# Four reads of scan states on GpSimd instead of VectorE, large loads held back, and new orders on all engines

## The chip, the cores and the metric

One Trainium2 chip, one of its cores. The metric is the device time of one execution in microseconds, taken as the median of several. The core has a matmul engine (TensorE, "PE" in the profile, its weight loads "PEld"), VectorE ("DVE"), ScalarE ("ACT"), GpSimd ("POOL") and SyncE ("SP", which here only issues transfers). Every engine runs its own list of instructions in the order in which it was written; semaphores tie the lists together.

## What is computed

Eight sequences of 256 tokens with 128 channels go through four layers, each followed by "add the input and normalize":

```python
x = _layernorm(x + attention(x))   # L0: linear attention, decay k, state kv by a scan over time
x = _layernorm(x + x @ W[idx] + b[idx])                    # L0 ffn, one expert out of 8
x = _layernorm(x + metric_attention(x))                    # L1: proj, gram, mixer
x = _layernorm(x + ffn(x))                                 # L1: silu(x w1)*(x w2), gelu(h1), gelu(h2), w3

# the attention of L0
k = sigmoid(x @ key_w.T + key_b); v, q = split(x @ vq_w.T)
upd = (1.0 - k)[..., :, None] * v[..., None, :]            # per head 8 x 8
_, kv = associative_scan(combine, (k[..., :, None], upd), axis=1)
h = einsum('nthd,nthde->nthe', q, kv);  return h @ out_w.T + out_b
```

The expert index comes from the logits and a noise vector, so its weights can only be fetched once a short chain of tiny operations is done.

## The kernel before

The 2048 tokens are cut into four groups (a, b, c or g = 0 to 3) of 512 columns, two sequences each. A group passes through these steps, and the groups overlap: while one group is in the last layer's feed-forward part, the next are still in the attention.

- **Attention, for each of eight value channels e.** TensorE spreads one row of value differences over 128 partitions (`replicate(a, e)`, bank `rep_bank`, two of them in turn). VectorE scans it over time (`scan(a, e)`: two instructions of 256 columns, into one of four buffers of `state`). The result is multiplied by the query (`read_state(a, e)`, 128x512, both inputs in SBUF, into one of four buffers of `read`). TensorE multiplies it with the output weights (`attend(a, e)`, eight matmul rows in the profile, summed in `y1_bank`). `direct_product(a)` and `attend_direct(a)` close the sum. `value_steps(a)`, `high_values`/`low_values(a, i)` make the value differences and split them in two parts. A scan may start when the read four steps back has ended (`STATES = 4`), a read when the attend four steps back has.
- **Normalization n of group g** (n = 0 to 2 inside, 3 at the end): `norm_sum`, `norm_stats`, `norm_moments`, `norm_varied` on VectorE, `inverse_std` on GpSimd (a power on 128x4, rows `rstd<-varied,power`), `norm_shift` on VectorE, `norm_out` on ScalarE (four tiles of 128 columns) for groups 0 and 1, on VectorE later. TensorE transposes the four tiles as they come (`transposes(g, n)`).
- **Expert layer.** VectorE and ScalarE take turns in `routing` and `route_on(0..7)`; after `route_on(7)` SyncE fetches `chosen_w` and `chosen_b`, GpSimd adds the identity (`passed_weights`), TensorE multiplies (`routed(b)`), and `norm_sum(1, b)` follows.
- **Metric layer.** `heads_of`, `gram_of`, `mask_gram`, `mix`, `through_metric`, `residual_of_metric`, `metric_out` go to and fro between TensorE, ScalarE and VectorE, then `norm_sum(2, b)`.
- **Feed-forward.** After `transposes(b, 2)`, ScalarE copies the high part (`high_x3`), VectorE takes the low part (`low_x3`), and TensorE runs `gate_of`/`up_of(c, m)` (rows with `x3T_high`, `x3T_low`), two hidden layers `hidden(c, layer, m)` of eight matmuls each, and `narrow(c)`, `turn_back(c)`. Every operand is in a high and a low part; GpSimd makes some of the low parts (`low_product`, `low_gelu`). The table of silu and that of gelu are loaded on ScalarE at each change (`ACT_TABLE_LOAD`).

GpSimd also adds the bias to the input (`attend_residual(a)`, row `res<-xt,attend_pack`), which needs the tokens `xt` from a transfer. SyncE issues all loads at the start in one go, and the reloads of `xt` later. In `without_weights()` TensorE does the work ahead of the first feed-forward matmul, in `with_weights()` the rest. The order of each engine is a list of calls at the end of its block: the four lists decide everything about who waits for whom.

## Time and profile before

| | us |
|---|---|
| median of 3 runs | 200.31 |
| lowest, highest | 199.05, 201.71 |
| profiled execution, whole | 198.95 |
| its span, first to last instruction | 197.2 |
| TensorE busy | 178.5 (91%) |
| VectorE busy | 143.8 (73%) |
| ScalarE busy | 124.7 (63%) |
| GpSimd busy | 63.9 (32%) |

A row of the timeline reads: start, duration, engine, line of the kernel, operation, output and inputs, and in brackets the idle time just before and what ended it. Rows of pipelined engines overlap by some 0.08 us, so what an instruction costs its engine is the distance of two starts, not the duration shown.

### The profile page before, as it was taken

To read this page: it belongs to the slowest core of one execution; us is meant where nothing else is said; L and a number is where in the kernel's file an instruction comes from. 1 tells how busy PE (TensorE), PEld (TensorE's weight loads), DVE (VectorE), ACT (ScalarE), POOL (GpSimd) and SP (SyncE) were. 2 spreads that over 40 slices of the span, in tenths; PEclk is the share of its full clock that TensorE was granted. 3 is DMA by queue.
4 is the path that set the end of the run, shared out by engine and by line. 5 is a ranking of instruction groups with operands and counts; after the bars stand their busy time and mean duration, and the time that the engine had idled before them with its cause. 6 is when DMAs were issued, how large, how long until landed. Compare 5 with 4: busy or idle time off the path is not lost.

```text
span 197.2 us, 2885 instructions
## 1 busy us (share of the span) xinstructions
PE 178.5 (91%) x949; PEld 140.4 (71%) x949; DVE 143.8 (73%) x375; ACT 124.7 (63%) x207; POOL 63.9 (32%) x61
## 2 busy tenths in 40 slices
PE   7797999698799999999999999999999999899940
PEld 7454685385697687997789889987678886576830
DVE  0699999989799999499779991777860545803572
ACT  3879972845304797635884663467877569885630
POOL 0020001420001152843504234490516572465511
PEclk9999999998899999999999999999999999999997
DMA  4998000210000000100000000000000100001102
GB/s 118 243 421 366 3 2 22 76 38 3 0 0 0 2 3 0 49 8 0 0 0 2 3 0 0 0 0 0 3 2 0 53 5 0 0 6 48 53 3 57
DMA packets 6704, 7.83 MB, mean 40 GB/s; under 512 B 544, under 2 KB 5664, under 8 KB 6432
## 3 DMA queue, kind: packets, MB, share of 16 engines
q1 hardware_dynamic: 6688, 7.63, 11.7%
q8 instruction: 9, 0.15, 0.3%
q14 instruction: 7, 0.06, 0.1%
HBM read 6.58 MB, written 1.05 MB: 39 GB/s over the span
## 4 chain that ended last, share of the span: by engine, by line
PE 56%; issue 15%; DVE 9%; ACT 9%; DMA 3%; POOL 3%; SPq 2%; POOLq 0%; DVEq 0%; ACTq 0%
PE c_bank L1386 33%; PE y_bank L1291 6%; PE b_bank L1320 6%; DMA xt<-x_tok 3%; ACT normed_lent L417 3%; PE b_bank L1347 2%; DVE state L832 2%; PE b_bank L1315 2%; SPq L239 1%; POOL res L293 1%; DVE stats L875 1%; PE b_bank L1386 1%; DVE read L842 1%; ACT gate L528 1%; PE sum_bank L1386 1%
## 5 line engine op out<-in xcount | busy, mean ns | idle before, releaser
L832 DVE TENSOR_TENSOR_SCAN state<-rep_bank,keep 128x256 f32<-128x256 f32 x62 | 38.8, 673 | 0.3 <-PE rep_bank L1278 0.3
L305 POOL TENSOR_TENSOR rstd<-varied,power 128x4 f32<-128x4 f32 x15 | 15.2, 1010 | 62.5 <-DVE varied L889 62.5
L1291 PEld LDWEIGHTS y_bank<-attend_pack,read 128*128 128x128 f32 x256 | 31.5, 192 | 5.0 <-DVE read L842 2.6
L1291 PE MATMUL y_bank<-attend_pack,read 128*128 128x128 f32 x256 | 33.1, 277 | 0.5 <-DVE read L842 0.3
L842 DVE TENSOR_TENSOR read<-state,query 128x512 f32<-128x512 f32 x32 | 22.4, 707 | 0.1
L314 POOL TENSOR_TENSOR hid_odd_low<-hid,hid_odd_high 128x512 fp32r<-128x512 f32 x12 | 15.7, 1311 | 20.2 <-ACT hid L545 20.1
L545 ACT ACTIVATE hid<-c_bank,scales_pack 128x512 f32<-128x512 f32 x31 | 21.0, 682 | 0.0
L1386 PE MATMUL c_bank<-hid_even_high,hidden_rounded 128*128 128x512 f32 x64 | 19.4, 414 | 0.5 <-ACT gate L528 0.5
L1386 PE MATMUL c_bank<-hid_odd_low,hidden_rounded 128*128 128x512 f32 x64 | 18.6, 400 | 0.5 <-DVE hid_odd_low L985 0.5
L1386 PE MATMUL c_bank<-hid_odd_high,hidden_rounded 128*128 128x512 f32 x64 | 18.7, 404 | 0.2 <-ACT hid L545 0.2
L539 ACT ACTIVATE hid_even_high<-c_bank,scales_pack 128x512 fp32r<-128x512 f32 x15 | 10.3, 688 | 13.2 <-PE c_bank L1386 13.1
L539 ACT ACTIVATE hid_odd_high<-c_bank,scales_pack 128x512 fp32r<-128x512 f32 x16 | 11.0, 688 | 11.8 <-PE c_bank L1386 11.6
L1386 PE MATMUL c_bank<-hid_even_low,hidden_rounded 128*128 128x512 f32 x64 | 18.4, 396 | 0.0
L309 POOL TENSOR_TENSOR hid_even_low<-hid,hid_even_high 128x512 fp32r<-128x512 f32 x8 | 10.2, 1283 | 21.0 <-ACT hid_even_high L534 21.0
L1386 PEld LDWEIGHTS c_bank<-hid_odd_low,hidden_rounded 128*128 128x128 f32 x64 | 12.0, 187 | 4.2 <-DVE hid_odd_low L985 1.4
L1386 PEld LDWEIGHTS c_bank<-hid_even_high,hidden_rounded 128*128 128x128 f32 x64 | 11.6, 189 | 3.9 <-ACT gate L528 0.9
L1386 PEld LDWEIGHTS c_bank<-hid_even_low,hidden_rounded 128*128 128x128 f32 x64 | 12.0, 188 | 3.2 <-DVE hid_even_low L980 0.4
L1386 PEld LDWEIGHTS c_bank<-hid_odd_high,hidden_rounded 128*128 128x128 f32 x64 | 11.5, 188 | 2.6 <-ACT hid L545 0.4
L417 ACT ACTIVATE normed_lent<-normed_lent,shift,rstd 128x128 f32<-128x128 f32 x16 | 6.6, 482 | 7.4 <-DVE shift L895 7.4
L314 POOL TENSOR_TENSOR hid_even_low<-hid,hid_even_high 128x512 fp32r<-128x512 f32 x8 | 10.3, 1293 | 2.5 <-ACT hid L545 2.5
L534 ACT CAST hid_even_high<-hid 128x512 fp32r<-128x512 f32 x16 | 9.7, 619 | 2.1 <-DVE hid L975 1.9
L293 POOL TENSOR_TENSOR res<-xt,attend_pack 128x512 f32<-128x512 f32 x4 | 5.6, 1408 | 15.0 <-DMA xt<-x_tok 13.1
(188 smaller groups left out, 361.7 us busy)
## 6 DMA issues: line engine op xcount, KB each, us to landing
hidden_pack<-hidden SPq DMA_DIRECT2D x2, 1024.0 KB, 10.5
xt<-x_tok SPq DMA_DIRECT2D x4, 256.0 KB, 2.8
xT_lent<-x_chan SPq DMA_DIRECT2D x3, 256.0 KB, 5.9
mlp_pack<-mlp SPq DMA_DIRECT2D x1, 768.0 KB, 7.7
out<-xT_lent SPq DMA_DIRECT2D x3, 256.0 KB, 2.3
attend_pack<-attend SPq DMA_DIRECT2D x1, 640.0 KB, 4.2
metric_pack<-metric SPq DMA_DIRECT2D x1, 448.0 KB, 11.8
xT_lent<-x_chan SPq DMA_DIRECT2D x2, 128.0 KB, 2.5
```

The costliest lines, as they stand in the source:

```text
L305: nc.gpsimd.tensor_tensor(rstd[n][:], varied[n][:], power[:], ALU.pow).then_inc(ln_rstd[n], 1)
L309: nc.gpsimd.tensor_tensor(hid_parts[0][1][:, m, :], hid[:, m, :], hid_parts[0][0][:, m, :].bitcast(F32), ALU.subtract).then_inc(low_pool[0 ...
L314: nc.gpsimd.tensor_tensor(hid_parts[layer][1][:, m, :], hid[:, m, :], hid_parts[layer][0][:, m, :].bitcast(F32), ALU.subtract).then_inc(lo ...
L417: nc.scalar.activation(normed[n][:, tile(j)], total[n][:, tile(j)], ACT.Identity, bias=shift[n][:, j:j + 1], scale=rstd[n][:, j:j + 1]).th ...
L534: nc.scalar.copy(hid_parts[0][0][:, m, :], hid[:, m, :]).then_inc(product_high, 1)
L539: nc.scalar.activation(hid_parts[layer][0][:, m, :], c_bank[m % 2][:], ACT.Gelu, scale=scale).then_inc(gelu_high, 1)
L545: nc.scalar.activation(hid[:, m, :], c_bank[m % 2][:], ACT.Gelu, scale=scale).then_inc(gelu_done, 1)
L832: ins = nc.vector.tensor_tensor_scan(state[:, e % STATES, at], rep_bank[e % 2][:, at], keep[:, a * T + s * SEQ:a * T + (s + 1) * SEQ], 0.0 ...
L842: nc.vector.tensor_tensor(read[:, e % READS, :], state[:, e % STATES, :], query[:, a * T:(a + 1) * T], ALU.mult).then_inc(read_ready, 1)
L1291: ins = nc.tensor.matmul(y1_bank[:, tile(j)], read[:, e % READS, tile(j)], out_w_rep_sb[:, e, :], start=(e == 0 and j == 0), stop=False, s ...
L1320: ins = nc.tensor.matmul(bank_[:, tile(j)], src[:, tile(j)], w(j), start=True, stop=True)
L1386: return nc.tensor.matmul(bank_[:], weights[exact[0]][k], moving, start=(k == 0 and i == 0), stop=(k == last and i == 1))
```

## The change

GpSimd makes four reads of states: (1, 2), (1, 5), (2, 2) and (2, 5). They have a semaphore of their own, and those who wait for a read ask `read_done` which one to wait for. At the start SyncE issues the tokens of group 0 after the second group's input, waits until that input has landed, and only then issues the remaining inputs, and the weights, `metric` first. A table `ACT_TILES` splits the tiles of `norm_out`; its values leave all four tiles with ScalarE where they were. The lists of calls of all engines are new.

```diff
+ACT_TILES = {(0, 0): 4, (0, 1): 4, (1, 0): 4, (1, 1): 4, (2, 0): 4, (2, 1): 4}
+POOL_READS = ((1, 2), (1, 5), (2, 2), (2, 5))
+        def read_done(a, e):
+            n = sum((i, k) in POOL_READS for i in range(a + 1) for k in range(HD if i < a else e + 1))
+            return (read_ready_pool, n) if (a, e) in POOL_READS else (read_ready, HD * a + e + 1 - n)
             for g in range(1, NG):
                 at = slice(g * T, (g + 1) * T)
                 sp.dma_start(xT[:, at], x_chan[:, at]).then_inc(xT_loaded[g], 16)
-            load_tokens(0)
-            for pack in ("mlp", "hidden1", "hidden2", "metric"):
+                if g == 1:
+                    load_tokens(0)
+                    sp.wait_ge(xT_loaded[1], 16)
+            for pack in ("metric", "mlp", "hidden1", "hidden2"):
                 load_pack(pack)
+            def read_state(a, e):                                    # on GpSimd
+                pool.wait_ge(scan_done, HD * a + e + 1)
+                pool.wait_ge(proj_out, PROJECTIONS * (a + 1))
+                if HD * a + e >= READS:
+                    pool.wait_ge(attended, HD * a + e + 1 - READS)
+                nc.gpsimd.tensor_tensor(read[:, e % READS, :], state[:, e % STATES, :], query[:, a * T:(a + 1) * T],
+                                        ALU.mult).then_inc(read_ready_pool, 1)
 # scan(a, e) on VectorE
-                    dve.wait_ge(read_ready, HD * a + e + 1 - STATES)
+                    dve.wait_ge(*read_done(*divmod(HD * a + e - STATES, HD)))
 # attend(a, e) on TensorE
-                pe.wait_ge(read_ready, HD * a + e + 1)
+                pe.wait_ge(*read_done(a, e))
 # VectorE's list, two of its places
             norm_varied(2, 0)
             norm_sum(0, 1)
             rounding_flag()
+            norm_stats(0, 1)
+            norm_shift(2, 0)
...
 # ScalarE's list, one of its places
+            sum_low_halves(2)
+            round_weights(2)
             norm_out(2, 0)
 # TensorE's list, the start
-                project(3)
                 replicate(0, 1)
                 replicate(0, 2)
+                project(3)
 # TensorE's list, the end
                 narrow_early(0)
+                narrow_early(1)
                 narrow_late(0)
-                narrow_early(1)
+                narrow_late(1)
                 turn_back_last(0)
-                narrow_late(1)
```

The list of GpSimd from the first `inverse_std` on, before. The `res` is `attend_residual(1)`, `passed_w` is `passed_weights`:

```order
L305 TENSOR_TENSOR rstd<-varied,power 128x4
L293 TENSOR_TENSOR res<-xt,attend_pack 128x512
L299 TENSOR_TENSOR passed_w<-chosen_w,metric_pack 128x128
L305 TENSOR_TENSOR rstd<-varied,power 128x4 x3
L309 TENSOR_TENSOR hid_even_low<-hid,hid_even_high 128x512 x2
```

The same place after. The reads stand between the powers of the normalizations:

```order
L347 TENSOR_TENSOR rstd<-varied,power 128x4
L333 TENSOR_TENSOR passed_w<-chosen_w,metric_pack 128x128
L327 TENSOR_TENSOR res<-xt,attend_pack 128x512
L340 TENSOR_TENSOR read<-state,query 128x512
L347 TENSOR_TENSOR rstd<-varied,power 128x4
L340 TENSOR_TENSOR read<-state,query 128x512 x2
L347 TENSOR_TENSOR rstd<-varied,power 128x4 x2
L351 TENSOR_TENSOR hid_even_low<-hid,hid_even_high 128x512
```

`passed_weights` has moved ahead of `attend_residual(1)`, and three reads stand in front of the first low part.

VectorE from the last step of the expert choice to the statistics of normalization 1 of group 0, before:

```order
L771 TENSOR_SCALAR expert<-route 128x1
L875 BN_STATS stats<-total 128x6 x4
L882 BN_AGGR moments<-stats 128x2 x4
L842 TENSOR_TENSOR read<-state,query 128x512
L889 TENSOR_SCALAR varied<-moments 128x4
L832 SCALAR_TENSOR_TENSOR state<-rep_bank,keep 128x256 x2
L895 SCALAR_TENSOR_TENSOR shift<-moments,rstd 128x4
L832 SCALAR_TENSOR_TENSOR state<-rep_bank,keep 128x256 x4
L842 TENSOR_TENSOR read<-state,query 128x512
L813 TENSOR_TENSOR dvalue_first<-dvalue,dvalue_first 64x512
L860 TENSOR_TENSOR normed_lent<-b_bank,chosen_b 128x512
```

After (the two reads in one row are (1, 1) and (1, 3)):

```order
L817 TENSOR_SCALAR expert<-route 128x1
L937 TENSOR_SCALAR varied<-moments 128x4
L888 TENSOR_TENSOR read<-state,query 128x512
L878 SCALAR_TENSOR_TENSOR state<-rep_bank,keep 128x256 x2
L943 SCALAR_TENSOR_TENSOR shift<-moments,rstd 128x4
L853 TENSOR_TENSOR dvalue<-value 128x512
L878 SCALAR_TENSOR_TENSOR state<-rep_bank,keep 128x256 x2
L888 TENSOR_TENSOR read<-state,query 128x512 x2
L878 SCALAR_TENSOR_TENSOR state<-rep_bank,keep 128x256 x2
L908 TENSOR_TENSOR normed_lent<-b_bank,chosen_b 128x512
```

The statistics now come before the last step of the choice, the low part of group 2's values has moved back, and two reads stand where one stood.

TensorE at the change from group 2 to group 3 in the feed-forward part, before (the `normed` transposes are `transposes(3, 2)`, the row of `mlp_rounded` with `hid_even_high` begins `narrow(2)`):

```order
L1315 MATMUL b_bank<-metric_pack,normed_lent 128x128 x4
L1386 MATMUL c_bank<-hid_odd_high,hidden_rounded 128x512 x4
L1386 MATMUL c_bank<-hid_odd_low,hidden_rounded 128x512 x4
L1386 MATMUL sum_bank<-x3T_high,mlp_rounded 128x512
L1386 MATMUL sum_bank<-x3T_low,mlp_rounded 128x512
L1386 MATMUL c_bank<-hid_even_high,mlp_rounded 128x512 x3
```

After:

```order
L1430 MATMUL c_bank<-hid_odd_high,hidden_rounded 128x512 x4
L1430 MATMUL c_bank<-hid_odd_low,hidden_rounded 128x512 x4
L1359 MATMUL b_bank<-metric_pack,normed_lent 128x128 x4
L1430 MATMUL c_bank<-hid_even_high,mlp_rounded 128x512 x3
L1430 MATMUL c_bank<-hid_even_low,mlp_rounded 128x512 x2
L1430 MATMUL c_bank<-hid_even_high,mlp_rounded 128x512
L1430 MATMUL c_bank<-hid_even_low,mlp_rounded 128x512 x2
L1430 MATMUL sum_bank<-x3T_high,mlp_rounded 128x512
```

The transposes stand behind the last hidden tile of group 2 now, and `narrow(2)` ahead of the first gate.

## Rows read from the trace of the kernel before

**Rows 1.** The page's second part: busy tenths in 40 slices of 4.93 us.

```profile
PE   7797999698799999999999999999999999899940
DVE  0699999989799999499779991777860545803572
```

**Rows 2.** Busy time (instructions) of each engine by stretch, then granted clock, DMA share, GB/s.

```profile
44.20:58.80 14.60, 12.64 (x72) 10.18 (x73) 13.08 (x33) 4.68 (x9) 0.00 (x0) 0.88 0.00 1
63.90:101.70 37.80, 37.36 (x206) 30.67 (x207) 32.74 (x81) 27.25 (x48) 15.99 (x13) 1.00 0.03 8
101.70:162.30 60.60, 59.79 (x342) 50.19 (x341) 40.07 (x123) 38.38 (x63) 27.20 (x23) 1.00 0.02 6
```

**Rows 3.** Timeline of VectorE: distance of starts, a wait for TensorE's replicate.

```profile
24.51 0.67 DVE L842 TENSOR_TENSOR read<-state,query 128x512 f32<-128x512 f32 x1
25.09 0.15 DVE L761 TENSOR_REDUCE route<-route 128x1 f32<-128x8 f32 x1
...
11.67 2.44 DVE L832 TENSOR_TENSOR_SCAN state<-rep_bank,keep 128x256 f32<-128x256 f32 x4 [0.29 <-PE rep_bank L1278]
```

**Rows 4.** Timeline of VectorE beside GpSimd, 36 to 40 us and at 80 us.

```profile
37.28 1.07 DVE L842 TENSOR_TENSOR read<-state,query 128x512 f32<-128x512 f32 x1
38.38 0.83 DVE L813 TENSOR_TENSOR dvalue_first<-dvalue,dvalue_first 64x512 fp32r<-64x512 f32 x1
39.91 0.69 DVE L860 TENSOR_TENSOR normed_lent<-b_bank,chosen_b 128x512 f32<-128x512 f32 x1 [0.71 <-PE b_bank L1320]
...
79.74 0.67 DVE L842 TENSOR_TENSOR read<-state,query 128x512 f32<-128x512 f32 x1
...
36.54 1.26 POOL L293 TENSOR_TENSOR res<-xt,attend_pack 128x512 f32<-128x512 f32 x1 [1.75 <-DMA xt<-x_tok]
37.76 0.90 POOL L299 TENSOR_TENSOR passed_w<-chosen_w,metric_pack 128x128 f32<-128x128 f32 x1
...
79.76 1.81 POOL L293 TENSOR_TENSOR res<-xt,attend_pack 128x512 f32<-128x512 f32 x1
```

**Rows 5.** Timeline of SyncE and TensorE around the expert's weights.

```profile
33.26 0.38 SPq L262 DMA_DIRECT2D chosen_b<-ffn_b  x1
...
38.72 1.16 PE L1320 MATMUL b_bank<-passed_w,x1T 128*128 128x128 f32 x8 [1.67 <-POOL passed_w L299]
```

**Rows 6.** TensorE in one microsecond (busy, granted clock), and VectorE's wait for the gram.

```profile
45.00:46.00 1.00, 0.91 (x3) 1.00 0.00 0
48.00:49.00 1.00, 1.00 (x6) 0.50 0.06 16
...
51.36 0.42 DVE L956 TENSOR_TENSOR gram<-b_bank,metric_pack 128x256 f32<-128x256 f32 x1 [1.42 <-PE b_bank L1347]
```

**Rows 7.** Timeline of ScalarE and VectorE where the feed-forward part starts.

```profile
60.30 1.65 ACT L417 ACTIVATE normed_lent<-normed_lent,shift,rstd 128x128 f32<-128x128 f32 x4 [5.76 <-DVE shift L895]
...
63.21 0.66 DVE L966 TENSOR_TENSOR x3T_low<-b_bank,x3T_high 128x512 fp32r<-128x512 f32 x1
```

**Rows 8.** Timeline of TensorE: transposes that wait for tiles, and one that doesn't.

```profile
66.88 1.28 PE L1315 MATMUL b_bank<-metric_pack,normed 128*128 128x128 f32 x4
...
77.33 0.94 PE L1315 MATMUL b_bank<-metric_pack,normed_lent 128*128 128x128 f32 x4
...
160.02 0.60 PE L1315 MATMUL b_bank<-metric_pack,normed_lent 128*128 128x128 f32 x4
```

**Rows 9.** ScalarE and TensorE from group 2 to group 3 of the feed-forward part.

```profile
163.79 1.28 ACT L528 ACT_TABLE_LOAD   x1
...
169.99 1.01 PE L1386 MATMUL c_bank<-hid_even_high,hidden_rounded 128*128 128x512 f32 x3 [0.51 <-ACT gate L528]
```

**Rows 10.** Timeline of ScalarE: the casts of both hidden layers' weights.

```profile
20.45 3.69 ACT L478 CAST hidden_rounded<-hidden_pack 128x2048 fp32r<-128x2048 f32 x2
```

**Rows 11.** Timeline of the last instructions: TensorE's wait, the last power on GpSimd.

```profile
187.87 0.39 PE L1481 MATMUL c_bank<-hid_even_low,mlp_rounded 128*128 128x256 f32 x1 [0.44 <-DVE hid_even_low L915]
...
192.19 0.73 POOL L334 TENSOR_TENSOR rstd<-varied,power 128x2 f32<-128x2 f32 x1 [0.67 <-DVE varied L944]
```

More of the change, by code:

```diff
@@ L713, in _ @@
             silu(3, 1)
-            silu_table(3)
             silu(3, 2)
@@ L1594, in with_weights @@
[L1594 to L1595 removed]
+                replicate(2, 7)
                 attend(2, 4)
+                transposes(1, 1)
                 attend(2, 5)
[L1598 to L1599 removed]
+                heads_of(1)
                 hidden(0, 1, 0)
+                gram_of(1)
                 hidden(0, 1, 1)
[L1602 removed]
+                mix(1)
+                hidden(0, 1, 2)
                 replicate(3, 0)
[L1604 removed]
```

468 lines of the change are left out of this document (238 added, 230 removed).

## The prediction

> **What bounds the kernel now.** I read the busy tenths first. VectorE stands at 9 with few breaks from 10 to 80 us while TensorE has 7s and 8s in between; from 80 us on TensorE stands at 9 to the tail and VectorE falls to 3 to 8 [rows 1]. The table by stretch says the same: from 63.9 to 101.7 us TensorE is busy 37.36 of 37.80, from 101.7 to 162.3 us 59.79 of 60.60 [rows 2]. So there are two halves. Up to the first feed-forward matmul VectorE is the bound (scans and reads), and what lies on its list ahead of `low_x3(0)` (start 63.21 [rows 7]) sets when TensorE's solid half begins. From there TensorE's fixed amount of work sets the end. A microsecond taken from VectorE ahead of 63 us is worth a microsecond if TensorE can be fed in the second half; one taken after is worth little.
>
> Then I read where VectorE stood still or was slow in the first half. It waited 0.29 us at 11.67 for a replicate [rows 3], 0.71 us at 39.91 for `routed(0)` and 1.42 us at 51.36 for the gram [rows 4, 6]. Two instructions ran long: a read of 1.07 us and a low part of 0.83 us [rows 4].
>
> **The sum, first half (up to `low_x3(0)`).**
> - Reads. Of the four, (1, 2), (1, 5) and (2, 2) stood ahead of `low_x3(0)`. A read costs VectorE 25.09 - 24.51 = 0.58 us [rows 3], in dense stretches 0.60; three give 1.8. On GpSimd a 128x512 product of two SBUF operands takes about 1.26 us, as the `res` row does [rows 4], and GpSimd was idle for the whole of 44.2 to 58.8 us [rows 2]. Their users (the scan four steps on, the attend) come over 2 us later in the new list, so the longer read is hidden; without that cover each would cost 0.7.
> - The wait of 0.29. In the new list `replicate(0, 1)` and `(0, 2)` stand ahead of `project(3)`, which waited for the second group's input. Gone: 0.29. I cost the holding back of the large loads at nothing: the input it may speed up is no longer waited for, and the first user of what is held back, ScalarE's cast of the `mlp` weights, feeds only the feed-forward part 40 us later.
> - The wait of 0.71. TensorE waited 1.67 us for `passed_w` until 38.72 [rows 5]; the weights had been asked for at 33.26, but GpSimd had first to wait for the tokens (`res`, 36.54, released by a transfer) [rows 4, 5]. With `passed_weights` in front, it starts some 1.8 us after the request, at 35, and `routed(0)` follows ScalarE's copy at about 36.4. Gone: 0.71.
> - The wait of 1.42. `heads_of(0)` and `gram_of(0)` ran at a granted clock of 0.50 (1.2 GHz, against 1.00 before), after microseconds in which TensorE had little to do [rows 6]. In the new list an attend stands between `transposes(0, 1)` and `heads_of(0)`, and VectorE has two scans, two reads, a direct product and a low part to do ahead of `mask_gram(0)`, where before there was less. Even at the slow clock the gram would be there. Gone: 1.42.
> - Contention as it was: 1.07 - 0.67 and 0.83 - 0.69 = 0.54 [rows 4]. Gone at its old place, since the neighbours change.
> - Against that, `norm_varied` and `norm_shift(0, 1)` now stand ahead of `low_x3(0)`: 0.15.
> - New contention. The read at 37.28 asked while GpSimd's `res` (36.54, 1.26 long) ran, and ended 0.55 us after that one had; at 79.76 it is `res` that takes 1.81 us, behind a VectorE read begun at 79.74 [rows 4]. So of two instructions with two SBUF inputs each, the later waits for the whole of the earlier. The Trainium skill has this as a rule (SBUF — State Buffer, "Who interferes with whom"): a VectorE instruction with two SBUF inputs contends with a GpSimd instruction that reads SBUF, and the loser blocks fully. By that rule the trace agrees, and it speaks against this change. Where does it bite? By the new list, `passed_w` would run about 34.9 to 35.8 and `res` 36.3 to 37.5, while VectorE wants its reads (1, 1) at 35.3 and (1, 3) at 36.3: 0.45 and 1.15. The moved reads mostly face scans, statistics and PSUM operands, which GpSimd doesn't slow; `read(2, 2)` falls together with VectorE's `read(2, 1)`, but starts later and so is the one that waits. I take 1.1, between 0 (VectorE is first each time) and 1.6.
>
> Sum: 1.8 + 0.29 + 0.71 + 1.42 + 0.54 - 0.15 - 1.1 = **3.5 us** (3.0 to 4.6). I set this against the list walked through with the distances of starts: the first shift would come at 33.4, that of normalization 2 at 57 instead of 60.1, and `high_x3(0)` 2.8 to 3.7 us earlier.
>
> **The sum, second half.**
> - `replicate(2, 5)` has moved behind the start: TensorE has 0.24 us more to do.
> - Waits of transposes for ScalarE's tiles. Four transposes take 0.60 as a row when the tiles are there, and took 1.28 at 66.88 and 0.94 at 77.33 [rows 8]; with the small idle pieces and another at 94.67 I count 1.7 us lost by TensorE between 63.9 and 101.7. In the new list `norm_out(1, 1)` comes ahead of the gelus and `norm_shift(1, 1)` some 8 us earlier, so that one goes; `norm_out(0, 1)` still is waited for (0.4), and `norm_out(2, 1)` (0.2). With a reserve I take a gain of 0.8 (0 to 1.2).
> - From group 2 to 3. ScalarE's table load ends at 165.07 and TensorE waits 0.51 for a gate at 169.99 [rows 9]. `high_x3(3)` now stands in that chain (0.6 longer), but TensorE's transposes have moved into the gap (0.36 shorter), and `narrow(2)` covers the copy. I take 0, between -0.6 and 0.4.
> - The tail. `narrow_early(1)` fills the 0.44 us that TensorE waited; the chain there runs on VectorE and GpSimd (the last power starts at 192.19) and gains 0.1 [rows 11].
> - Everything between 101.7 and 162.3: TensorE idles 0.81 in all [rows 2]. The new orders could hardly win there; I take nothing.
>
> 3.5 - 0.24 + 0.8 + 0 + 0.1 = 4.16, **4.2 us**. The profiled execution took 198.95 (span 197.2), so it becomes 194.8. That execution is the lowest of four readings (198.95, 199.05, 200.31, 201.71), whose middle is 199.7; from there 195.5, from the median of the runs, 200.31, it would be 196.1. I say **195.5**.
>
> **The rivals.**
> - *Only the reads count.* VectorE is still over 90% busy from 60 to 80 us [rows 1], and the time won at its waits reappears as other waits of the new list, since the chain of layers (shift, ScalarE, transposes, GpSimd) has lengths of its own. Then four reads at 0.6 are left, 2.4, less 0.24: 2.2 us, 197.5 us. For it: half of my gain is waits, and waits move. Against: each has its cause removed by name.
> - *The shared access eats the gain.* Each GpSimd read blocks a VectorE instruction for its whole 1.26 us, and is itself late: 4 x 1.26 = 5.0 against 5.3 (the 4.2 with its 1.1 of contention left out): 199.4 us. Against: VectorE's neighbours there are mostly scans, which ran beside GpSimd unslowed.
> - *The other side: ScalarE in front of the chain.* Before, both casts of the hidden weights were done by 24.1 (3.69 us, [rows 10]). Now one stands ahead of `norm_out(1, 0)` with a table load, the other with its sum of halves between `move_mixed(0)` and `norm_out(2, 0)`: 1.85 + 1.28, and 1.85 + about 1.9 (an estimate: the sum reads as much as the cast). If norm 1's shift comes before 40.3 and norm 2's before 54, they are in the chain; fully exposed that is 6.9 against the 4.2: 202.4, and beyond 2% with a wait of the flag (`flag_sum` needs that sum) on top, 204. Against: ScalarE waited 5.76 us ahead of `norm_out(2, 0)` [rows 7], and by my walk the slack is 2 and 3 us. It decides only from there.
> - *More than I count*: no contention and all waits of the transposes gone, 4.6 - 0.24 + 1.2 + 0.4 + 0.1 = 6.1 us: 193.6.
>
> **Chances.** Forecast (gain 3.2 to 5.2) 0.48; only the reads 0.22; shared access 0.15; ScalarE's side 0.07, of which two thirds beyond 2%; more 0.08. The range reaches from "more" (193.6, and 0.8 below it for the scatter of the four readings) up to the shared access at 199.4. 2%, about what a measurement of this kernel can tell from no change, is a gain of 4.0, just below the forecast: faster 0.50, same 0.45, slower 0.05.
>
> **What would show it.** In the changed kernel's timeline: `passed_w` at 35 and ahead of the second `res`; no VectorE wait above 0.3 us at the gram; GpSimd reads of 1.3 us, VectorE reads of over 1 us only beside `res` or `passed_w`; `norm_out(2, 0)` at about 57 and `high_x3(0)` near 59.5 instead of 62.4; a granted clock of 1.00 from 45 to 52; TensorE busy over 98% from there on. I am wrong if VectorE's reads last over a microsecond at several places, if ScalarE comes to `norm_out(2, 0)` straight from a cast, or if TensorE idles more than 1 us between 60 and 160.

## The result, and the profile after

The changed kernel takes 193.62 us (192.63 to 194.08, four executions) where the kernel before, run beside it, took 200.38 (199.05 to 201.71): a ratio of 0.972, 95% interval 0.967 to 0.977. Run again later, beside the kernel before on one chip, it took 193.77 (192.90 to 195.75, six executions) against 198.68: 0.978 (0.973 to 0.982). One of those seventeen executions of the kernel before took 251.57 us, at a mean granted clock of 0.655, and is left out of the ratio. The profiled execution took 193.92 us, span 192.1; the one before had 198.95 and 197.2.

The busy tenths and the granted clock (the share of its full speed at which TensorE ran), page of the kernel after:

```profile
PE   7779796999999999999999999999899999999930
DVE  0799999999999997679979986668470774804461
PEclk9999999999999999999999999999999999999985
```

TensorE's long row of 9s begins at the 8th slice (34 us) instead of the 12th (54 us); VectorE's has no break from the 3rd to the 15th, where there were two, in the 9th and 11th [rows 1]. The same in windows of the kernel after (busy time and count of PE, PEld, DVE, ACT, POOL, then granted clock, DMA share, GB/s), the three stretches that answer to [rows 2]:

```profile
39.00:53.60 14.60, 13.87 (x101) 11.93 (x99) 14.44 (x36) 8.55 (x13) 3.94 (x3) 1.00 0.02 6
59.20:97.00 37.80, 37.75 (x211) 31.49 (x212) 32.69 (x76) 27.82 (x49) 14.74 (x13) 1.00 0.03 8
97.00:155.80 58.80, 57.87 (x332) 48.42 (x331) 42.21 (x122) 37.05 (x60) 28.19 (x23) 1.00 0.02 6
```

In the first one VectorE is busy 14.44 of 14.60 (13.08 before) and the clock is 1.00 (0.88 before); in the second TensorE idles 0.05 us where it idled 0.44.

The timeline of GpSimd and VectorE in the kernel after, where [rows 4] and [rows 6] were:

```profile
34.42 0.46 POOL L333 TENSOR_TENSOR passed_w<-chosen_w,metric_pack 128x128 f32<-128x128 f32 x1 [1.83 <-DMA chosen_b<-ffn_b]
35.83 1.34 POOL L327 TENSOR_TENSOR res<-xt,attend_pack 128x512 f32<-128x512 f32 x1 [0.94 <-DMA xt<-x_tok]
37.12 1.28 POOL L340 TENSOR_TENSOR read<-state,query 128x512 f32<-128x512 f32 x1
...
34.65 1.38 DVE L888 TENSOR_TENSOR read<-state,query 128x512 f32<-128x512 f32 x2
37.14 0.66 DVE L908 TENSOR_TENSOR normed_lent<-b_bank,chosen_b 128x512 f32<-128x512 f32 x1
46.72 0.40 DVE L1004 TENSOR_TENSOR gram<-b_bank,metric_pack 128x256 f32<-128x256 f32 x1
```

The weights come ahead of the residual and take 0.46 us instead of 0.90; neither `norm_sum(1, 0)` (37.14) nor the gram's mask (46.72) has a wait behind it. At the start of the feed-forward part, ScalarE and VectorE, for [rows 7]:

```profile
55.41 1.65 ACT L463 ACTIVATE normed_lent<-normed_lent,shift,rstd 128x128 f32<-128x128 f32 x4 [3.24 <-DVE shift L943]
...
58.45 0.69 DVE L1014 TENSOR_TENSOR x3T_low<-b_bank,x3T_high 128x512 fp32r<-128x512 f32 x1
```

`low_x3(0)` starts at 58.45 instead of 63.21, 4.76 us earlier. Then TensorE at the turn from group 2 to 3 and the last power on GpSimd, for [rows 8, 9, 11]:

```profile
156.34 0.60 PE L1359 MATMUL b_bank<-metric_pack,normed_lent 128*128 128x128 f32 x4
...
161.05 0.50 PE L1430 MATMUL c_bank<-x3T_high,mlp_rounded 128*128 128x512 f32 x1 [0.42 <-ACT gate L612]
...
186.58 0.73 POOL L376 TENSOR_TENSOR rstd<-varied,power 128x2 f32<-128x2 f32 x1 [0.23 <-DVE varied L992]
```

The lead at the last power is 5.61 us; the span shows 5.1.

**Where the two ends of an execution lie.** To compare profiles of many kernels one has to leave out two stretches that differ from execution to execution of one kernel. Ahead, VectorE's first scan starts when the first transfers and ScalarE's copies are done: at 8.18 us here, at 9.00 in a second profile of the same kernel. Behind, the output's last transfer: from the end of VectorE's last instruction to the end of the span it took 4.15 us here and 2.22 in that second profile. So the table counts from the start of the first scan; all figures are starts on VectorE's timeline (the scan reads `sum_bank`; the last instruction is the last scaling of `xT_lent`).

| kernel | first scan at | to `low_x3(0)` | to last instruction | span |
|---|---|---|---|---|
| before | 8.49 | 54.72 | 184.47 | 197.2 |
| old orders, four reads on GpSimd | 8.27 | 54.53 | 184.32 | 196.8 |
| new orders, all reads on VectorE | 8.05 | 55.56 | 185.52 | 197.6 |
| the same, spare matmuls at 22 us | 8.20 | 53.05 | 183.03 | 194.1 |
| after | 8.18 | 50.27 | 179.17 | 192.1 |
| after, second profile | 9.00 | 50.42 | 179.28 | 191.1 |
| after, spare matmuls at 22 us | 8.24 | 50.18 | 179.08 | 191.5 |
| after, loads as before | 8.33 | 51.55 | 180.42 | 191.6 |
| after, five more reads on GpSimd | 10.28 | 49.98 | 179.30 | 193.5 |
| after, heads ahead of the attend | 8.41 | 52.96 | 181.83 | 194.0 |
| after, turn 2 to 3 as before | 8.22 | 50.21 | 180.23 | 192.6 |
| before, attend between | 8.65 | 53.72 | 183.48 | 196.7 |
| before, spare matmuls at 45 us | 8.03 | 54.14 | 183.88 | 196.5 |
| before, weights first | 8.17 | 53.74 | 183.54 | 196.2 |

Seven of these fourteen profiles, the one of the kernel before among them, hold a fall of TensorE's granted clock ahead of `low_x3(0)`: about 1 us of a difference between two rows can be that and nothing else.

Before to after that is 4.45 us in the first half, 0.85 in the second, 0.31 at the start, and 0.52 given back behind the last instruction: 5.1 in the span.

### The profile page after: what moved, and what is told of

It is laid out like the page before. It is cut to its first block and busy times, and to the rows that moved or that the text cites. A ratio compares the mean times of both kernels' runs of the same rounds, so it can differ in the third digit from the quotient of the medians.

```text
span 192.1 us, 2885 instructions
## 1 busy us (share of the span) xinstructions
PE 173.9 (91%) x949; PEld 138.1 (72%) x949; DVE 143.7 (75%) x371; ACT 124.9 (65%) x207; POOL 69.6 (36%) x65
## 3 DMA queue, kind: packets, MB, share of 16 engines
HBM read 6.58 MB, written 1.05 MB: 40 GB/s over the span
## 5 line engine op out<-in xcount | busy, mean ns | idle before, releaser
L347 POOL TENSOR_TENSOR rstd<-varied,power 128x4 f32<-128x4 f32 x15 | 15.9, 1063 | 57.0 <-DVE varied L937 57.0
L888 DVE TENSOR_TENSOR read<-state,query 128x512 f32<-128x512 f32 x28 | 20.8, 754 | 0.0
L1322 PE MATMUL rep_bank<-dvalue_second,rep_r 128*128 128x512 f32 x16 | 8.3, 524 | 2.2 <-DVE state L878 1.5
```

The costliest lines, as they stand in the source:

```text
L347: nc.gpsimd.tensor_tensor(rstd[n][:], varied[n][:], power[:], ALU.pow).then_inc(ln_rstd[n], 1)
L888: nc.vector.tensor_tensor(read[:, e % READS, :], state[:, e % STATES, :], query[:, a * T:(a + 1) * T], ALU.mult).then_inc(read_ready, 1)
L1322: nc.tensor.matmul(rep_bank[e % 2][:], rep_r[:, e, :], dvalue_parts[a % 2][e // (HD // 2)][:], start=True, stop=True).then_inc(rep_ready, 1)
```

## The experiments

**Reads alone, orders alone.** First the four reads on GpSimd in the old lists, with the loads as before:

```diff
 # VectorE's list, four places
-            read_state(1, 2)
 # GpSimd's list
             passed_weights()
+            read_state(1, 2)
             inverse_std(1, 0)
+            read_state(1, 5)
+            read_state(2, 2)
...
             inverse_std(0, 1)
+            read_state(2, 5)
```

> The lists of the kernel before, with only the four reads moved to GpSimd (in the places that suit that list); loads as before. Theory A (orders make the gain: each VectorE wait ends at a fixed event of another engine, so a read taken away ahead of a wait only makes the wait longer): reads (1,2) and (1,5) are swallowed by the waits at 39.9 and 51.4, (2,2) counts 0.6: low_x3(0) starts at about 62.6 instead of 63.2, time 0.6 us under the kernel before (ratio 0.997). Theory B (only the reads count, 0.6 us each): low_x3(0) at 61.4, time 1.8 to 2.2 us less (ratio 0.989). Theory C (shared access of VectorE and GpSimd eats it): no gain or a loss, ratio 1.00 to 1.01, VectorE instructions of over 1 us beside the GpSimd reads.

198.03 us, ratio 0.993 (0.988 to 0.998). VectorE's timeline in it, for the two waits of [rows 4, 6]:

```profile
39.74 0.69 DVE L905 TENSOR_TENSOR normed_lent<-b_bank,chosen_b 128x512 f32<-128x512 f32 x1 [1.57 <-PE b_bank L1361]
51.18 0.42 DVE L1001 TENSOR_TENSOR gram<-b_bank,metric_pack 128x256 f32<-128x256 f32 x1 [2.02 <-PE b_bank L1388]
```

The waits of 0.71 and 1.42 have become 1.57 and 2.02 (both profiles have the clock down at 48 us), and there is a new one of 0.29 at `low_x3(0)`, for ScalarE. VectorE does 1.8 us less and stands 1.75 us longer; in the profile 0.2 us is left at `low_x3(0)`. The freed time is swallowed where VectorE waits for others. That is one execution of each kernel. Over all of them the gain is larger: a ratio of 0.993 of 199 us is 1.3 us, with an interval from 0.4 to 2.3, so it lies between the 0.6 of theory A and the 2.2 of theory B and excludes neither.

Then the new lists and the held loads, with the four reads back on VectorE:

```diff
-POOL_READS = ((1, 2), (1, 5), (2, 2), (2, 5))
+POOL_READS = ()
 # VectorE's list, one of four places
             read_state(1, 1)
+            read_state(1, 2)
             read_state(1, 3)
```

> The changed kernel with the four reads given back to VectorE, all else new. Theory A: VectorE of the changed kernel has no wait between 10 and 58 us, so three reads ahead of low_x3(0) cost it their full 0.6 each: low_x3(0) at 60.2 instead of 58.45, the time 1.8 us above the changed kernel (about 195.4 where that has 193.6; ratio to the kernel before 0.981). Theory B (orders bring nothing without the reads): back to the time of the kernel before, ratio 0.995 to 1.0. Theory C (the reads on GpSimd cost as much as they save): the same time as the changed kernel, ratio 0.972.

199.08 us, ratio 0.998 (0.993 to 1.002): nothing of the gain can be told from noise. What was lost is more than the 1.8 us of the three reads on the path, and the trace names a cause that I had not thought of. TensorE's attends and VectorE in this kernel, then the windows of TensorE's clock:

```profile
24.46 4.57 PE L1335 MATMUL y_bank<-attend_pack,read 128*128 128x128 f32 x24
...
29.96 0.69 DVE L911 TENSOR_TENSOR total<-y_bank,res 128x512 f32<-128x512 f32 x1 [1.30 <-PE y_bank L1342]
...
22.00:24.00 2.00, 0.59 (x2) 0.31 (x2) 2.00 (x6) 2.00 (x3) 0.00 (x0) 1.00 0.08 25
24.00:26.00 2.00, 1.92 (x11) 1.60 (x12) 2.00 (x5) 1.71 (x4) 0.00 (x0) 0.77 0.01 4
26.00:28.00 2.00, 2.00 (x11) 2.00 (x11) 2.00 (x5) 0.00 (x0) 0.00 (x0) 0.50 0.00 0
```

TensorE has little to do from 22 to 24 us (busy 0.59 of 2.00), its clock then reads 0.77 and 0.50 (1.2 GHz instead of 2.4 for most of three microseconds), 24 attend matmuls take 4.57 us (3.03 in the changed kernel's profile), and VectorE waits 1.30 for their result. At 46 to 48 us the clock reads 0.50 again. Of its ten executions eight have a mean clock of 0.967 to 0.977, lower than any of the changed kernel's.

**Does the clock do it?** Six spare matmuls in TensorE's gaps, their result used by nobody; the same edit in this kernel and in the changed one:

```diff
+            def keep_busy():
+                for _ in range(2):
+                    nc.tensor.matmul(b4_bank[:, 0:P], ones[:], ones[:], start=True, stop=True)
 # TensorE's list
+                keep_busy()
                 replicate(1, 0)
+                keep_busy()
                 replicate(1, 1)
+                keep_busy()
                 attend(0, 5)
```

> New orders with the four reads on VectorE, and the same six spare matmuls in the gap at 22 to 24 us. Without them this kernel had clock 0.77 and 0.50 from 24 to 28, `attend(0, 5..7)` in 4.57 us, and `norm_sum(0, 0)` waited 1.30 us for TensorE; `low_x3(0)` came at 63.61. Theory Clock: 1.00 from 24 to 28, that wait under 0.2, `low_x3(0)` near 62.2, time about 197.6 (ratio 0.991). What is left against the changed kernel (some 3.5 us) is then the price of the reads themselves and of the second dip at 46 to 50. Rival: the dip comes from something else; times as without the spare matmuls, 199 and ratio 0.998.

> The changed kernel with six spare 128x128 matmuls of the constant `ones` on TensorE, two each ahead of `replicate(1, 0)`, `replicate(1, 1)` and `attend(0, 5)`, where TensorE has the three short waits around 22 to 24 us (0.66 and 0.68 us in the changed kernel's trace). Their result is not used. Theory Clock: with TensorE only 0.96 busy in the 2 us from 22, the granted clock stands at an edge; in the run with the old loads the same gap was followed by 0.60 and 0.54, and the 24 matmuls of `attend(0, 5..7)` took 4.57 us where they take 3.03. Spare work in the gap keeps the clock at 1.00, the scatter between executions shrinks, and the median falls by some 0.5 us (as if no execution had the dip, worth about 1.3). Rival: the clock does not follow the gap, or VectorE is the bound there anyway; the spare matmuls (about 0.24 us each) then cost 0 to 0.5 us, same clock in the runs as before.

With the reads on VectorE: 197.53 us, ratio 0.994 (0.990 to 0.998), against 199.08 without the spare work. Its TensorE timeline:

```profile
24.27 2.84 PE L1339 MATMUL y_bank<-attend_pack,read 128*128 128x128 f32 x24
```

4.57 has become 2.84 and the wait of 1.30 is gone. So the wait was the slow clock. That the spare matmuls kept the clock up is likely and not shown by the profile alone: in the one without them the `mlp` weights had also landed later (18.57 instead of 17.93), VectorE had waited 0.58 us for what is queued behind them, and part of TensorE's thin stretch came from that (0.96 busy of the 2 us in the changed kernel, 0.59 here). The profile with them is also of the fastest of its ten executions, 195.85. The mean clocks of all executions say more: eight of ten are at 0.977 or below without the spare work, two of ten with it. In the changed kernel the window answering to the one above is

```profile
22.00:24.00 2.00, 1.54 (x10) 1.15 (x9) 2.00 (x6) 1.98 (x3) 0.00 (x0) 1.00 0.05 12
```

(0.96 busy without the spare work). It took 193.35 us, four executions within 193.27 to 193.66, ratio 0.972 (0.965 to 0.979). In the profile it is 0.1 us shorter than the changed kernel, which had no fall of the clock in its own profile either. The narrow spread is what the theory asked for, but the median is not apart from 193.62 or 193.77, and with no fall in the profile of either there is nothing here that the spare work can be seen to prevent.

The two kernels with spare matmuls have no fall ahead of `low_x3(0)` and no wait of VectorE between its first scan and there. They give the price of the reads in the new lists: 53.05 to 50.18 at `low_x3(0)`, 2.87 us, and 183.03 to 179.08 at the end, 3.95 us. Three reads at 0.60 are 1.8 of the 2.87. The rest stands on two rows of the kernel with the reads on VectorE:

```profile
34.67 2.95 DVE L884 TENSOR_TENSOR read<-state,query 128x512 f32<-128x512 f32 x3
...
35.75 1.32 POOL L327 TENSOR_TENSOR res<-xt,attend_pack 128x512 f32<-128x512 f32 x1 [1.09 <-DMA xt<-x_tok]
...
69.00 1.23 DVE L939 SCALAR_TENSOR_TENSOR shift<-moments,rstd 128x4 f32<-128x4 f32 x1
```

Reads (1, 1), (1, 2) and (1, 3) take 2.88 us from start to start instead of 1.8, because the last of them meets GpSimd's `res`: 1.08 us of shared access. With (1, 2) moved away VectorE has two reads there and is out before it matters (1.31 us in the profile of after, 1.20 in the one with spare matmuls). So the moved read takes its own 0.6 and a meeting of 1.1 with it. Behind `low_x3(0)` there is the fourth read, and a step of 128x4 that lasts 1.23 instead of 0.16 beside a GpSimd product (third row).

In the old lists the same four reads were worth 0.2 in the profile. And the new lists without them are worth 1.4 (184.47 to 183.03). 0.15 and 1.44 make 1.6; together they made 5.3. (The 1.44 and the 5.3 both hold about 1 us that the kernel before lost in its profile to a fallen clock, below.) These are single executions. By the ratios, the reads alone bring 0.7%, the lists alone 0.2% (0.6% with the spare matmuls), and both together 2.2 and 2.8% in the two comparisons: a smaller disproportion than in the profiles, and still about twice the sum. The change is neither half but the two together.

**The same kernel again.**

> The changed kernel itself once more, beside the others on one chip, for the scatter of its executions: the version with spare matmuls at 22 to 24 us stayed within 193.27 to 193.66. Theory Clock: this one scatters by 1 us or more, with a median 0 to 0.6 above 193.35. Rival: the spare matmuls changed nothing; same median and same narrow spread.

192.90 to 195.75, six executions, median 193.77; mean clock 0.981 to 0.992, the longest at 0.981. The scatter is over 1 us, as expected of it; the median is 0.4 above the one with spare work, on another chip, which settles nothing.

**The loads.** The changed kernel with SyncE's requests in the order before:

```diff
-                if g == 1:
-                    load_tokens(0)
-                    sp.wait_ge(xT_loaded[1], 16)
-            for pack in ("metric", "mlp", "hidden1", "hidden2"):
+            load_tokens(0)
+            for pack in ("mlp", "hidden1", "hidden2", "metric"):
```

> The changed kernel with SyncE's start as it was: nothing held back, tokens after all inputs, mlp before metric. As predicted (holding back is worth nothing): same times to 0.1 us, low_x3(0) at 58.4, the time that of the changed kernel. Rival E (holding back brings the earlier start: the first VectorE scan of pair (0,1) stood at 9.37 in the changed kernel and the first scans 0.5 us earlier than before): the first value steps at 6.5 go back to 7.1, low_x3(0) 0.5 us later, the time 0.5 us more.

193.60 us, ratio 0.974 (0.966 to 0.983): no difference. But its profile isn't the same, it has the fall of the clock, in the same place:

```profile
24.19 4.57 PE L1332 MATMUL y_bank<-attend_pack,read 128*128 128x128 f32 x24
```

VectorE waits 1.30 us for it, which is all of its 1.3 us at `low_x3(0)`. It seems to belong to that execution (mean clock 0.973; the other three have 0.984 to 0.987). The rival of an earlier start falls: the second value step stands at 6.63 with the old loads, at 6.49 and 7.31 in two profiles with the held ones. I had costed the held loads at nothing because ScalarE's cast of the `mlp` weights feeds only the feed-forward part. That overlooks what is queued behind the cast: ScalarE's cast of `dvalue_first`, which VectorE needs for its low part. With the old loads the first cast started at 15.67 without waiting; in the changed kernel it waited 2.01 us, to 17.65, and VectorE's low part found its input with half a microsecond to spare. Two other executions with held loads did not (below).

**More reads.** Five more on GpSimd: (0, 1), (0, 3), (0, 5), (1, 6), (1, 7).

```diff
-POOL_READS = ((1, 2), (1, 5), (2, 2), (2, 5))
+POOL_READS = ((0, 1), (0, 3), (0, 5), (1, 2), (1, 5), (1, 6), (1, 7), (2, 2), (2, 5))
 # GpSimd's list
             attend_residual(0)
+            read_state(0, 1)
+            read_state(0, 3)
+            read_state(0, 5)
...
             read_state(1, 5)
+            read_state(1, 6)
+            read_state(1, 7)
             read_state(2, 2)
```

> The changed kernel with five more reads on GpSimd: (0,1), (0,3), (0,5), (1,6), (1,7), lists otherwise as they are. Theory A (VectorE is the only bound up to 58 us): 5 x 0.6 = 3.0 us less ahead of low_x3(0), which starts at 55.5; the time 3.0 us under the changed kernel, 190.6. Rival D (a second chain, shift - ScalarE - transposes - heads - gram, or TensorE's own list, lies just behind VectorE): VectorE gets waits of together 1.5 us or more, the gain is 0.5 to 1.5 us. Theory C (shared access): GpSimd's nine reads at 1.27 us block VectorE reads, gain below 0.5 us.

194.45 us, ratio 0.975 (0.966 to 0.984). From the first scan on, 50.0 us to `low_x3(0)` and 179.3 to the end, against 50.3 and 179.2: VectorE has 3 us less to do and gets 0.3 of it, for a while. VectorE and GpSimd in this kernel:

```profile
16.55 1.13 DVE L808 TENSOR_SCALAR route<-route 128x8 f32<-128x8 f32 x1
45.61 1.20 DVE L864 TENSOR_TENSOR dvalue_first<-dvalue,dvalue_first 64x512 fp32r<-64x512 f32 x1
47.41 1.27 DVE L883 TENSOR_TENSOR_SCAN state<-rep_bank,keep 128x256 f32<-128x256 f32 x2 [0.60 <-PE rep_bank L1322]
...
15.87 1.77 POOL L340 TENSOR_TENSOR read<-state,query 128x512 f32<-128x512 f32 x1 [1.81 <-DVE state L883]
44.99 1.27 POOL L340 TENSOR_TENSOR read<-state,query 128x512 f32<-128x512 f32 x1 [0.57 <-PE y_bank L1335]
```

A step of 128x8 elements that takes 0.23 us elsewhere lasts 1.13, beside a GpSimd read that itself lasts 1.77; the low part at 45.61 ends 0.55 us behind the read that began at 44.99. Then VectorE waits for TensorE (0.60, and 0.44 at `through`). At these two rows shared access takes 1.4 us of the three; two reads of 0.82 take another 0.3, and the waits 1.0. So the rival I feared is real; it is four reads in the right places that escape it.

**The place of the attend and the clock at 45 to 50 us.** In the changed kernel, the attend moved behind the heads:

```diff
                 transposes(0, 1)
-                attend(1, 3)
                 heads_of(0)
+                attend(1, 3)
```

> The changed kernel with `heads_of(0)` ahead of `attend(1, 3)` on TensorE, so that this attend no longer lies in the wait for ScalarE's copy. Theory A/Clock: TensorE is idle 0.6 us more at 44 to 46, heads wait for the copy either way; the chain is no later (gram within 0.1 of 46.72), the attend moves behind it; the clock is at 1.00 in most executions but dips to 0.50 in some between 46 and 50, a median 0 to 0.6 us above the changed kernel. Rival (the place of the attend is what saved the 1.42 us): the gram waits again by 0.5 us or more in the profile at clock 1.00.

194.54 us (193.84 to 195.91), ratio 0.978 (0.973 to 0.983). From `total(0)` to `low_x3(0)` its profile has 30.52 us, the changed kernel's 30.30: no wait at the gram, at a clock of 1.00. So the attend's place is not what removed it. The median is not apart from the 193.77 of the changed kernel beside it. The profile was of the longest of the four executions; ScalarE and VectorE in it:

```profile
19.56 1.47 ACT L524 CAST mlp_rounded<-mlp_pack 128x1536 fp32r<-128x1536 f32 x1 [3.70 <-DMA mlp_pack<-mlp]
...
21.59 0.69 DVE L859 TENSOR_TENSOR dvalue_first<-dvalue,dvalue_first 64x512 fp32r<-64x512 f32 x1 [1.19 <-ACT dvalue_first L504]
30.85 0.69 DVE L915 TENSOR_TENSOR total<-y_bank,res 128x512 f32<-128x512 f32 x1 [1.19 <-PE y_bank L1342]
```

This is what the held loads can cost: `mlp` landed 1.9 us later than in the profile of after, ScalarE's cast held up the next, VectorE waited 1.19, TensorE starved for it (busy 0.28 of the 2 us from 22, by the windows), its clock fell to 0.50, and VectorE waited another 1.19. The kernel with all reads on VectorE shows the same, smaller: 0.58 us at 20.59.

In the kernel before, the attend put between:

```diff
                 flag_sum()
-                attend(1, 4)
                 replicate(1, 7)
                 transposes(0, 1)
+                attend(1, 4)
                 replicate(2, 0)
                 heads_of(0)
```

> The kernel before, with one move on TensorE: `attend(1, 4)` from ahead of `replicate(1, 7)` to between `transposes(0, 1)` and `heads_of(0)`, where TensorE waits for ScalarE. Theory A (the gram of group 0 waits for TensorE because this attend was in front of the chain): the chain's `heads_of(0)` comes some 0.5 us earlier, VectorE's wait of 1.42 us at the gram falls to 0.5 to 0.9, `low_x3(0)` 0.5 to 0.9 earlier, time 198.3 to 198.6 where before has 199.0. Theory Clock: what makes that wait is the clock of 0.50 at 48 to 50 us; if the move closes the idle stretch at 44 to 46 the clock stays at 1.00 and the wait goes altogether (1.4 us); if the clock still falls, the wait stays above 1 us.

198.18 us, ratio 0.999 (0.994 to 1.003). And in the kernel before, four spare matmuls:

```diff
+                keep_busy(b5_bank, 1)
                 transposes(0, 1)
                 replicate(2, 0)
+                keep_busy(b5_bank, 2)
                 heads_of(0)
                 replicate(2, 1)
+                keep_busy(b4_bank, 1)
                 gram_of(0)
```

> The kernel before with four spare 128x128 matmuls on TensorE: one ahead of `transposes(0, 1)`, two ahead of `heads_of(0)`, one ahead of `gram_of(0)`. Their results are not used; all else is as before. Theory Clock: in the trace of before the clock reads 0.86, 0.50 and 0.79 from 46 to 52 us, `heads_of(0)` took 1.79 us where 1.05 is usual, the gram's matmuls 1.76 where 1.16, and VectorE then waited 1.42 us. With the gaps filled the clock stays at 1.00, the wait falls to about 0.3 (the two stretched pieces make up 1.3, less some 0.1 to 0.3 for the spare work on the chain), `low_x3(0)` comes about 1 us earlier and the time is 198.0 to 198.4. Rival (order alone: the attend in front of the chain makes the wait, as I predicted): wait and time as before, 1.4 us and 199.0 to 199.3.

198.41 us, ratio 0.998 (0.995 to 1.001). Last, the kernel before with GpSimd's weights ahead of the residual:

```diff
-            attend_residual(1)
             passed_weights()
+            attend_residual(1)
```

> The kernel before with `passed_weights()` ahead of `attend_residual(1)` on GpSimd, nothing else. Before: residual 36.54, weights 37.76 (0.90 us), VectorE waits 0.71 us at 39.91 for what TensorE makes from them. Theory A: the weights come as soon as `chosen_b` is in, near 36.4, end near 37.2 and TensorE's `routed(0)` 1.1 to 1.4 us earlier; the residual is not wanted before the last part of group 1. The wait of 0.71 goes whole. Its gain is then given back at the gram, where TensorE is already late: `norm_sum(1, 0)` 0.7 us earlier, `low_x3(0)` 0 to 0.7 earlier. Rival: the transfer of `chosen_b` and not the order on GpSimd sets it; wait of 0.4 to 0.7 stays.

One execution of 197.94 us. The gram's row on VectorE's timeline in these three, in this order:

```profile
50.52 0.42 DVE L956 TENSOR_TENSOR gram<-b_bank,metric_pack 128x256 f32<-128x256 f32 x1 [0.37 <-PE b_bank L1347]
```

```profile
50.32 0.42 DVE L956 TENSOR_TENSOR gram<-b_bank,metric_pack 128x256 f32<-128x256 f32 x1 [0.36 <-PE b_bank L1352]
```

```profile
35.98 0.46 POOL L299 TENSOR_TENSOR passed_w<-chosen_w,metric_pack 128x128 f32<-128x128 f32 x1 [0.47 <-DMA chosen_b<-ffn_b]
...
39.85 0.69 DVE L860 TENSOR_TENSOR normed_lent<-b_bank,chosen_b 128x512 f32<-128x512 f32 x1
50.06 0.43 DVE L956 TENSOR_TENSOR gram<-b_bank,metric_pack 128x256 f32<-128x256 f32 x1 [0.18 <-PE b_bank L1347]
```

In all three the granted clock reads 1.00 from 44 to 52 us, and the wait that was 1.42 is 0.37, 0.36 and 0.18. The third changed nothing near the gram. So over 1 us of that wait was the clock of that one execution, not the order on TensorE. From `total(0)` to `low_x3(0)` before has 32.72 us and the three have 31.66, 31.67 and 30.69: 1.06 and 1.05 for the clock, and 2.03 in the third, which has no wait of 0.71 either. The weights' order is worth 0.97 in this one execution: the wait of 0.71 whole, and small pieces beside it; I had expected the gram to swallow part of it. (The table's 53.74 for this kernel hides that: its clock had fallen at 10 to 14 us, and VectorE waited 0.93 and 0.31 us for replicates, where before has 0.29.) The medians of the first two kernels can't be told from that of the kernel before, which fits a fall at 48 us that belongs to single executions.

Whether the spare work is what held the clock I can't say: in the kernel with it, TensorE's clock fell earlier instead, windows of that kernel:

```profile
38.00:40.00 2.00, 1.34 (x9) 1.34 (x10) 1.18 (x3) 1.95 (x3) 0.60 (x1) 0.90 0.44 135
40.00:42.00 2.00, 2.00 (x9) 1.81 (x9) 2.00 (x6) 1.11 (x3) 0.00 (x0) 0.50 0.00 1
```

after the same gap (busy 0.95 and 1.34 in the four microseconds from 36) that in the profile of before (0.94 and 1.28) was followed by 1.00. There it cost nothing, since the chain did not hang on TensorE. The same list of instructions shows a fall in one execution and none in another.

**The turn from group 2 to 3,** back as it was, in the changed kernel:

```diff
 # TensorE's list
-                hidden(2, 2, 3)
                 transposes(3, 2)
-                narrow(2)
+                hidden(2, 2, 3)
                 gate_of(3, 0)
+                narrow(2)
 # VectorE's list
             norm_out(2, 3)
+            norm_varied(3, 1)
+            low_x3(3)
             low_gelu(2, 2, 2)
             low_gelu(2, 2, 3)
-            low_x3(3)
-            norm_varied(3, 1)
```

(and `high_x3(3)` ahead of the last gelus of group 2 on ScalarE.)

> The changed kernel with the turn from group 2 to group 3 as before on three engines (`high_x3(3)` first on ScalarE, `low_x3(3)` and `norm_varied(3, 1)` first on VectorE, `transposes(3, 2)` ahead of `hidden(2, 2, 3)` on TensorE). The trace shows 5.87 us of lead at `hidden(2, 1, 0)` and 5.36 at `hidden(3, 1, 0)`. Theory A (the new turn costs what is lost there): the lead at `hidden(3, 1, 0)` is 5.8, time 0.3 to 0.5 us under the changed kernel, ratio about 0.970. Rival: TensorE is over 98% busy there either way and the half microsecond is lost in the matmuls' own pace; no difference, ratio 0.972 to 0.974.

194.87 us, ratio 0.979 (0.970 to 0.988). The profile is slower by 1.1 us behind that place, and by nothing ahead of it; the ratio's interval still overlaps that of the changed kernel with spare matmuls on the same chip (0.965 to 0.979). TensorE's timeline:

```profile
155.49 0.84 PE L1359 MATMUL b_bank<-metric_pack,normed_lent 128*128 128x128 f32 x3 [0.81 <-DVE normed_lent L957]
```

VectorE's `norm_out` of group 3 is not done when TensorE, now 5.9 us ahead, comes for it. My reading, that the new turn costs the half microsecond lost there, is wrong in its conclusion: from `hidden(2, 1, 0)` to `hidden(3, 1, 0)` it loses 0.5 of the lead, and the old one 1.7. Of both, 0.3 is lost well ahead of the turn, inside the first hidden layer of group 2 (two matmuls with `hid_even_low` take 0.89 us there, 0.63 before), so the turn itself costs 0.2 and the old one 1.4.

## Why the prediction came out as it did

195.5 us was forecast with a range of 192.8 to 199.4; it became 193.62. The forecast gain on the profiled execution was 4.2 us; it was 5.0. The medians lie 6.8 us apart in the first comparison and 4.9 in the second, where the kernel before came out 1.7 us lower. Direction and mechanism held, the size was short by a sixth, and some of its parts are right for another reason. Part of the closeness is luck: the contention was put too high by 1.0 us, and 1.05 us of the gain in the profile was a fall of the clock in one execution, which the sum counted as something that the new order removes. Without that fall in the profile of before the gain from first scan to last instruction is 5.3 - 1.05 = 4.25 us, and the two errors cancel to the 4.2 of the forecast.

- *VectorE sets the first half, TensorE the second.* Right. 4.45 us of the 5.3 between the first scan and the last instruction were won ahead of `low_x3(0)`, and TensorE was busy 37.75 of 37.80 us behind it.
- *Three reads, 1.8.* Right as a price, wrong as a term that stands alone. With the old lists the four were worth 0.2 us in the profile and 1.3 by the ratio; with the new ones they are worth 2.87 at `low_x3(0)`, of which 1.08 is shared access that the moved read avoids, and 3.95 at the end. The rival "only the reads count" (2.2 us in all) falls with the 4.9 to 6.8 us measured.
- *The wait of 0.71.* Right, with its cause: the run with nothing but the weights first takes the whole of it.
- *The wait of 1.42.* It went. But I put it among what the order on TensorE removes, beside the fallen clock; 1.05 of it was the fall alone, and it is missing in three other executions of nearly the same kernel (in a fourth, the old lists with four reads moved, it came again). The new lists take the remaining 0.2 to 0.4, and they have VectorE so busy that even a slow TensorE would be in time, as I argued.
- *New contention, 1.1.* The term that was mis-sized: it came to about 0.1 (`res` 1.34 instead of 1.26, VectorE's two reads 0.69 each, second read on GpSimd 1.28). My walk had VectorE's reads (1, 1) and (1, 3) at 35.3 and 36.3, each inside the run of `passed_w` or `res`; they ran from 34.65 to 35.96, nearly between the two, also because `passed_w` took 0.46 and not the 0.90 that I had copied. The size was right for the order that I had not asked about: with (1, 2) on VectorE too the same place costs 1.08. With 0.1 in its place the sum for the first half is 4.5; measured 4.45, the fall of 1.05 being in both.
- *Held loads at nothing.* Right in the median, and the reason given is false: they put a transfer in front of ScalarE's cast for VectorE, with 0.5 us to spare in one execution and 1.2 short in another.
- *ScalarE in front of the chain.* It waited 1.19 us for the first shift and 3.24 for the second (forecast slack 2 and 3); the rival was rightly small.
- *The second half.* 0.7 forecast, 0.85 found, so right in sum and less so in its parts: a lead of 4.73 at the first gate matmul grows to 5.86 at group 3's first transposes (+1.1; forecast 0.56), falls to 5.36 at `hidden(3, 1, 0)` (0.33 of it inside the first hidden layer of group 2, 0.18 at the turn, where a gate is waited for 0.42 us; forecast for the turn 0, from -0.6 to +0.4), and ends at 5.61 (+0.25; forecast 0.1). TensorE idled 1.00 of the 100 us from 60 to 160, just at the bound that I had named as a sign of being wrong (1.48 before).
- *The shared access as a rival.* The price per meeting was right, and five more reads pay it (0.9 and 0.5 us at the two rows). The Trainium skill's rule (SBUF — State Buffer, "Who interferes with whom") is about who blocks whom; by it these rows agree, the small step at 16.55 too, since that section counts `tensor_scalar`, with its one tensor input, among those that can contend when their operands meet certain conditions; no run shows whether this step meets them. My walk had looked only for instructions with two. How often two such instructions meet decided.
- *The 193.6 of "more than I count"* is the time it took, and that is chance too: it stood for a gain of 6.1 us, and the profile gained 5.0. Of its two conditions the contention did stay away, and the transposes gave their share; half a microsecond went back between the hidden layers of groups 2 and 3.

## What to carry to other kernels

Take work off the bounding engine and change the order together: alone, the one is largely swallowed at the next wait for the engine behind, and here the two were worth 0.7% and 0.2 to 0.6% apart and 2.2 to 2.8% together. Look too at what the moved instruction had pushed its neighbours into: here one read less on VectorE also saved a meeting of 1.1 us with GpSimd. Before a wait in a profile is given a cause in the code, look whether TensorE's granted clock was down in the microseconds ahead of it, and whether another execution shows the same; with spans, compare between two instructions inside the kernel and leave out the first and last transfer. And when a load is moved later, look not only for who uses it but for what stands behind its user in that engine's queue.

## What the hardware did that I had not expected

- One kernel's executions differ by some microseconds (before: 197.38 to 201.29 in nineteen on one chip, mean clock 0.967 to 0.994) for three reasons that the profiles show. TensorE's clock falls from 1.00 to 0.50 for some 3 us after it had little to do, in some executions and not in others: 24 attend matmuls in 4.57 us instead of 2.84, up to 1.3 us of waiting. The first scan starts between 8.03 and 9.00 us (10.28 once). The last write ends 2.2 to 4.2 us behind the last instruction.
- Nearly the same stretch ahead of it (TensorE busy 2.22 of 4 us, and 2.29) was followed by none in the first profile and by a fall in the second, so here a fall could not be told from the busy shares alone. The Trainium skill (TensorE: Matmul & The Clock Gate, Part 1) says that what sets the clock watches activity on a count of its own, which does not start with the kernel; that would fit the difference between executions, and no run here tests it. Spare matmuls in the gap at 22 us went with fewer low mean clocks in the kernel with all reads on VectorE (two of ten executions at 0.977 or below, instead of eight); in the changed kernel, which shows no fall in either of its profiles, nothing can be said, and in the kernel before the clock fell ahead of the place where the four spare ones stand.
- Not run: the changed kernel with the old loads and the spare matmuls together. By the profiles it should not have ScalarE's late cast, and if the spare work is what holds the clock, not the fall at 24 us either. Its best executions should be no better than the changed kernel's, which already have neither; an estimate, from the 0.1 us between the profiles with and without the spare work.
